# The head of a ternary 3x3 convolution: the weights loaded ahead of images 1 to 3, image 0's D, mean and variance taken ahead of the turning of the taps, image 1's mean and variance ahead of or between the first products

## What is computed

```python
max_val = jnp.max(jnp.abs(weight))
w_norm = weight / max_val                       # (1 where max_val is 0)
delta = 0.05 * jnp.max(jnp.abs(w_norm))
tern = where(w_norm > delta, 1, where(w_norm < -delta, -1, 0))
wq = where(tern > 0, Wp[0] * tern, where(tern < 0, Wn[0] * tern, tern))
...
g = x.reshape(B, 32, C // 32, H, W)
gn = ((g - mean(g)) / sqrt(var(g) + 1e-5)).reshape(x.shape)
out = x + conv3x3(gn, wq) + bias[None, :, None, None]
```

## Time and profile before

| | us |
|---|---|
| median of 3 runs | 574.85 (574.74 to 574.89) |
| time of the profiled execution | 575.64 |
| its span, first to last instruction | 574.0 |
| PE busy | 534.1 (93%) |
| DVE busy | 542.9 (95%) |
| ACT busy | 504.4 (88%) |
| POOL busy | 166.2 (29%) |

### The profile page before, as it was taken

The page is one execution under the profiler, slowest core; times in us unless marked ns, Lnnn a source line. Parts: engine busy times, 40 slices in busy tenths (PEclk is TensorE's granted clock), DMA queues, the critical chain, the costliest instruction groups (busy, mean ns, idle before and its releaser), DMA issues.

```text
span 574.0 us, 9367 instructions
## 1 busy us (share of the span) xinstructions
PE 534.1 (93%) x3238; PEld 320.1 (56%) x3238; DVE 542.9 (95%) x506; ACT 504.4 (88%) x485; POOL 166.2 (29%) x107
## 2 busy tenths in 40 slices
PE   0597999999999999999999999999999999999994
PEld 0453555555555555555555555565555555555552
...
DMA packets 28104, 153.43 MB, mean 267 GB/s; under 512 B 3504, under 2 KB 3504, under 8 KB 28080
## 3 DMA queue, kind: packets, MB, share of 16 engines
...
q10 hardware_dynamic: 576, 0.59, 0.3%
...
...
## 4 chain that ended last, share of the span: by engine, by line
DVE 68%; issue 24%; PE 4%; DMA 2%; DVEq 1%; ACT 1%; ACTq 0%
DVE parts L581 25%; DVE y L600 18%; DVE plane L541 10%; DVE plane L547 10%; DMA y<-in_L_conv_weight_dram 2%; PE even_rows L732 2%; DVE newton L570 2%; PE odd_rows L732 1%; DVEq L157 1%; DVE plane L553 1%; DVE neg_var L559 1%; ACT parts L386 1%; DVE rstd L565 0%; PE even_rows L697 0%; DVE parts L587 0%
## 5 line engine op out<-in xcount | busy, mean ns | idle before, releaser
L732 PE MATMUL odd_rows<-parts,w_lhsT 128*128 128x385 f16 (+1 forms) x1536 | 266.8, 330 | 8.6 <-DVE parts L581 7.5
L732 PE MATMUL even_rows<-parts,w_lhsT 128*128 128x385 f16 (+1 forms) x1536 | 267.6, 331 | 3.7 <-DVE parts L587 2.9
L581 DVE SCALAR_TENSOR_TENSOR parts<-plane,norm_scale,parts 128x1568 f16<-128x1568 f32 x127 | 233.4, 1842 | 4.3 <-ACT parts L386 4.3
L324 POOL TENSOR_TENSOR plane<-x 128x1512 f32<-128x1512 f32 x32 | 109.2, 3413 | 384.1 <-DVE parts L581 366.9
L732 PEld LDWEIGHTS even_rows<-parts,w_lhsT 128*128 128x128 f16 x1536 | 150.0, 98 | 111.9 <-issue 8.7
L732 PEld LDWEIGHTS odd_rows<-parts,w_lhsT 128*128 128x128 f16 x1536 | 148.1, 100 | 108.2 <-DVE parts L581 9.4
L386 ACT ACTIVATE parts<-plane,norm_scale 128x1568 f16<-128x1568 f32 x127 | 199.8, 1597 | 9.8 <-ACT plane L426 5.2
L432 ACT ACTIVATE junk<-x,negmean 128x3136 f16<-128x3136 f32 x32 | 92.9, 2904 | 0.0
L392 ACT ACTIVATE junk<-x 128x3136 f16<-128x3136 f32 x31 | 86.9, 2804 | 0.0
L600 DVE SCALAR_TENSOR_TENSOR y<-even_rows,out_scale,d_sb 128x784 f32<-128x784 f32 x62 | 61.0, 1025 | 0.0
L600 DVE SCALAR_TENSOR_TENSOR y<-odd_rows,out_scale,c_sb 128x784 f32<-128x784 f32 x62 | 60.9, 1023 | 0.0
...
## 6 DMA issues: line engine op xcount, KB each, us to landing
x<-in_x_dram SPq DMA_DIRECT2D x64, 784.0 KB, 11.7
...
y<-in_L_conv_weight_dram ACTq DMA_DIRECT2D x1, 576.0 KB, 10.7
wp_sb<-in_L_conv_Wp_dram ACTq DMA_DIRECT2D x1, 0.5 KB, 6.3
wn_sb<-in_L_conv_Wn_dram ACTq DMA_DIRECT2D x1, 0.5 KB, 7.9
...
```

The lines of the kernel that those rows point to most:

```text
L324: nc.gpsimd.tensor_tensor(plane[B][:, 0:PAIRS - 1, :], even[:, 0:PAIRS - 1, :], even[:, 1:, :], ALU.subtract).then_inc(plane_ready[B], 1)
L581: nc.vector.scalar_tensor_tensor(part(img, j, LO), plane[j][:], norm_scale[:, b_slice(img)], part(img, j, HI), ALU.mult, ALU.subtract).the ...
L732: ins = nc.tensor.matmul(product_ps(odd, b, b + 1)[:, 0, :, to:to + n], w_lhsT[:, prod, kw, :], part(img, prod, which)[:, b * BANK_ROWS:(b ...
```

## The change

The weights' DMA goes first in ACT's queue, ahead of Wp, Wn and the bias; SP issues image 0's loads and then waits for the weights before it issues those of images 1 to 3. DVE finds the local maximum, makes image 0's D and then the ternary weights; image 0's variance matmul stands ahead of the turning. ACT sums image 1 ahead of image 0's first high part, and PE's mean of image 1 stands behind the warm-up and ahead of all products. Image 0's A and B are both made by DVE, in the second slot; image 1's variance is taken in the middle of product D of image 0, and its A is moved to the third slot. The output scales and the comparison of Wp and Wn are placed anew, the negative weights are made only for the second pass, and the warm-up has 6 matmuls. Taps A and B are turned in other banks.

```diff
--- before.py
+++ after.py
@@
-WARM_UP = 11
+WARM_UP = 6
...
-            ps, bank = (odd_ps, 2) if j == B else (even_ps, j)
+            ps, bank = {C: (even_ps, 0), D: (even_ps, 1), A: (odd_ps, 1), B: (odd_ps, 2)}[j]
...
                             if img.buf != nxt.buf or img is nxt:
+                                if p == 0 and img is far:
+                                    sp.wait_ge(w_loaded, 16)
                                 load(img, 0, first=img is nxt)
                                 load(img, 1, first=img is nxt)
...
-                    if nxt:
-                        difference_b(nxt, after_c=now)
+                    if now and nxt:
+                        difference_b(nxt)
...
+            act.dma_start(w_raw, weight.rearrange("o i h w -> o (i h w)")).then_inc(w_loaded, 16)
             act.dma_start(wp_sb[:], wp.rearrange("(a b) -> a b", a=1).broadcast_to([P, 1])).then_inc(scalars_loaded, 16)
             act.dma_start(wn_sb[:], wn.rearrange("(a b) -> a b", a=1).broadcast_to([P, 1])).then_inc(scalars_loaded, 16)
-            act.dma_start(w_raw, weight.rearrange("o i h w -> o (i h w)")).then_inc(w_loaded, 16)
...
                         sum_squares(nxt)
                         edges(nxt)
                         root(nxt)
+                        sum_x(far)
                         make_first_hi(nxt)
                         make_hi(nxt, D)
+                    if second_slot:
+                        take_mean(nxt)
+                        sum_squares(nxt)
+                        make_hi(now, A)
+                        copy_c(now)
+                        make_hi(now, B)
+                        root(nxt)
+                        copy_d(now)
+                        make_hi(nxt, C)
                         sum_x(far)
-                    if now:
+                    elif now:
                         make_hi(now, A)
                         make_hi(now, B)
-                        if second_slot:
-                            take_mean(nxt)
                         copy_c(now)
-                        if second_slot:
-                            sum_squares(nxt)
-                        if nxt and not second_slot:
+                        if nxt:
                             root(nxt)
-                        if far and not second_slot:
+                        if far:
                             sum_x(far)
                         copy_d(now)
-                        if second_slot:
-                            root(nxt)
-                            sum_x(far)
...
+            def ternary_weights():
+                dve.wait_ge(w_max_turned, 1)
+                step(nc.vector.tensor_reduce(w_max[:], w_max_ps, AX_X, ALU.max))
+                step(nc.vector.tensor_scalar(col[0], w_max[:], 0.0, None, ALU.is_equal))
+                step(nc.vector.tensor_tensor(col[1], w_max[:], col[0], ALU.add))
+                step(nc.vector.reciprocal(col[2], col[1]))
+                nc.vector.tensor_scalar(w_raw, w_raw, col[2], None, ALU.mult)
+                step(nc.vector.tensor_scalar(col[3], w_max[:], col[2], THRESHOLD, ALU.mult, ALU.mult))
+                step(nc.vector.tensor_scalar(col[4], col[3], -1.0, None, ALU.mult))
+                dve.wait_ge(scalars_loaded, 32)
+                step(nc.vector.tensor_tensor(equal[:], wp_sb[:], wn_sb[:], ALU.is_equal))
+                step(nc.vector.tensor_scalar(neg, w_raw, col[4], equal[:], ALU.is_lt, ALU.mult))
+                nc.vector.scalar_tensor_tensor(pos, w_raw, col[3], neg, ALU.is_gt, ALU.subtract).then_inc(w_ternary, 1)
...
+                def make_first_b(img):
+                    plane_free(img, B)
+                    even = x_sb[img.buf][:, 0:H:2, :]
+                    nc.vector.tensor_tensor(plane[B][:, 0:PAIRS - 1, :], even[:, 0:PAIRS - 1, :], even[:, 1:, :],
+                                            ALU.subtract).then_inc(plane_ready[B], 1)
...
                 def emit(prev, now, nxt, far):
                     first_slot, second_slot = not now and not prev, now and not prev
                     if first_slot:
+                        if p == 0:
+                            local_max()
+                        make_d(nxt)
+                        if p == 0:
+                            ternary_weights()
+                        variance(nxt)
                         make_c(nxt)
-                        turned_weights((C, D))
-                        variance(nxt)
-                        turned_weights((A,))
                         first_rstd(nxt)
                         newton_factor(nxt)
                         scale_of_x(nxt)
-                        turned_weights((B,))
+                        turned_weights((C, D))
+                        make_first_lo(nxt)
+                    if second_slot:
+                        turned_weights((A, B))
+                        make_lo(now, D)
+                        make_a(now)
+                        make_first_b(now)
+                        variance(nxt)
+                        if p == 0:
+                            output_scales()
+                        make_lo(now, A)
+                        make_c(nxt)
+                        first_rstd(nxt)
+                        newton_factor(nxt)
+                        scale_of_x(nxt)
+                        make_lo(now, B)
                         make_d(nxt)
-                        make_first_lo(nxt)
-                        make_a(nxt)
-                    if now:
+                        make_lo(nxt, C)
+                    elif now:
+                        third_slot = prev.j == 0 and prev.q == p * N_IMG // X_BUFS
                         make_lo(now, D)
-                        if nxt and not second_slot:
+                        if third_slot:
+                            make_a(now)
+                        if nxt:
                             variance(nxt)
                         make_lo(now, A)
-                        if second_slot and p == 0:
-                            negative_weights()
-                    if now and nxt:
-                        make_c(nxt)
-                        make_d(nxt)
-                        if not second_slot:
+                        if nxt:
+                            make_c(nxt)
+                            make_d(nxt)
                             first_rstd(nxt)
                             newton_factor(nxt)
                             scale_of_x(nxt)
-                    if now:
                         make_lo(now, B)
-                    if now and nxt:
-                        make_a(nxt)
-                        if second_slot:
-                            variance(nxt)
-                            first_rstd(nxt)
-                            newton_factor(nxt)
-                            scale_of_x(nxt)
-                        make_lo(nxt, C)
+                        if nxt:
+                            make_a(nxt)
+                            make_lo(nxt, C)
...
                         if p == 0:
                             turn_max()
                         sum_first_mean(nxt)
-                        turn_weights()
                         pe.wait_ge(negmean_ready, nxt.count(plus=1))
                         sum_var(nxt, start=True)
+                        turn_weights()
                         warm_up()
+                        pe.wait_ge(var_ready, nxt.count(plus=1))
+                        sum_mean(far, start=True)
                     if second_slot:
-                        pe.wait_ge(w_ready, 4 * p + 4)
+                        pe.wait_ge(w_ready, 4 * p + 2)
                     if now:
                         if second_slot:
                             pe.wait_ge(half_lo_ready, p + 1)
@@ -766,18 +802,18 @@
                         multiply(now, C, 2)
                         multiply(now, C, 3)
                         wait(pe, odd_done, now.half(0))
-                        if second_slot:
-                            pe.wait_ge(var_ready, now.count(plus=1))
-                            sum_mean(nxt, start=True)
-                        elif nxt:
+                        if nxt and not second_slot:
                             sum_var(nxt, start=True)
                         pe.wait_ge(lo_ready[D], now.count(plus=1))
+                        if second_slot:
+                            pe.wait_ge(w_ready, 4 * p + 4)
                         multiply(now, D, 0)
                         multiply(now, D, 1)
-                        multiply(now, D, 2)
                         if second_slot:
                             pe.wait_ge(negmean_ready, nxt.count(plus=1))
-                        elif nxt:
+                            sum_var(nxt, start=True)
+                        multiply(now, D, 2)
+                        if nxt:
                             pe.wait_ge(var_ready, nxt.count(plus=1))
                         multiply(now, D, 3)
                         pe.wait_ge(lo_ready[A], now.count(plus=1))
@@ -786,15 +822,12 @@
```

(5 more changed lines are left out.)

45 lines of the change are left out of this document (21 added, 24 removed).

## The result

The changed kernel takes 566.77 us, the median of 4 runs (566.25 to 567.34), beside 574.81 us (574.74 to 574.89) for the kernel before; the ratio is 0.986, its 95% interval 0.9843 to 0.9877. The forecast was 566.3, in a range of 564.9 to 569.9. The profiled execution took 566.68 us over a span of 565.0.

The account below looks back on a forecast made before the run. DVE was taken as full from slot 1's middle to the end. Gains of 5.6 and 3.0 us took the span from 574.0 to 565.4, profiled time 567.0, less 0.79 for the median: 566.3 us, range 564.9 to 569.9.

Parts of the forecast that it names:

- Landing: DMA in the head: the weights land at 7.9 us (before 12.6) and the whole of image 0 at 9.8.
- my two bounds: Arrival of weights and whole image 0 by DMA: lower 7.1 and 9.1 us, upper 8.5 and 10.5.
- the loads come later: Rival, chance 0.14: image 1 or the weights arrive late by DMA; image 1 at 18.5 gives 568.3, weights at 10.4 cost 1.7.
- reference point: Start of DVE's low part of D of image 3: 86.85 us before the change, forecast 78.2.
- DVE to the ternary weights: Head on DVE: D(0) from 9.85 to 11.55, then the ternary chain; weights ready at 16.15 us, before 19.02.
- To the first product: Head on ACT and PE: first low half at 20.3, first product at 21.3 us (before 27.08), 5.6 us gained.
- First low half to the reference point: DVE's work from image 0's first low half to D(3)'s low part: 57.9 us, before 60.9, 3.0 gained.
- The new stall: In image 1's slot, DVE waits 1.65 us for ACT's high part of A after A(1) ends at 45.2.
- Sum: Whole kernel: 5.6 before the first product plus 3.0 after the first low half, 8.6 us off the span, to 565.4.
- The lower clock after the new wait: Rival, chance 0.15: PE idles from 47.7 to 49.9, then runs at half speed; about 3.0 us reach DVE, 568 to 569.7.
- No change: Rival, chance 0.02: in the slots, DVE is not what a slot waits for, so the time stays the same.
- slower: Rival, chance 0.02: in the head, image 1 queued behind the weights lands after 25.1 us, 17 us after issue.

Follow-up runs that it names:

- a_first_warm9: Changed kernel with plane A of image 1 made ahead of the low part of D in the third slot, and nine warm-up matmuls, not six; 564.55 us, ratio 0.9807.

## Why the prediction was right

*Landing.* Forecast 7.9 and 9.8, measured 7.6 and 9.4. Both lie between my two bounds, 0.3 and 0.4 us earlier than the middle that I took; the repeat of the same kernel landed at 8.2 and 10.0, so the middle lies between the two executions. The estimate beside it, by the Trainium skill, "DMA: Bandwidth & Descriptors", section "Anatomy of one DMA — SWDGE (gpsimd) path", was 8.0 for both together; the page gives its formula for DMAs issued by GpSimd, these were issued by SP and ACT, and 9.4 was measured. The rival "the loads come later" didn't come: nothing of PE waited for image 1's mean. The wait in SP's queue was not without effect, though; I had given it no gain, and without it the reference point comes 1.4 us later.

*DVE to the ternary weights.* Forecast 16.15, measured 15.69 (14.27 + 1.42), by the earlier landing. D(0) took 1.79, as I took it, and not 2.14.

*To the first product.* Forecast: squares done 15.6, variance 16.25, first low half 20.3, first product 21.3. Measured: 15.4, 16.10, 20.17, 21.35. The 0.4 of the earlier landing shrank on the way, since the mean matmuls and copies, an estimate of 1.15, took 1.38 (10.98 to 12.36). The mis-sized term here is the warm-up: 1.3 us forecast, 2.12 measured, since I scaled a row at the higher level and this one ran at the lower. It ends at 20.57 and the first product was wanted at 21.3, so the slack hid it.

*First low half to the reference point.* Forecast 57.9 us, measured 58.02 (78.19 - 20.17); low D(1) at 41.56 for 41.7, low D(2) at 61.57 for 61.6. The new stall, 1.65, came as forecast, and PE's wait behind it was 2.26 for the 2.2 between 47.7 and 49.9. In a_first_warm9, which makes A(1) ahead of the low part, that wait of DVE is gone.

*Slots.* 16.62 both before and after.

*Sum.* Forecast 8.6, measured 8.66 at the reference point, 9.0 in the span: the last output row of DVE starts 8.62 earlier (557.62 for 566.24), and the rest is the end of the stores. The profiled time is 566.68 where 567.0 was forecast. I then took off 0.79, since the median of before stood that far below its profile; after the change median and profile agree within 0.1 us. On the three chips of the experiments the kernel before has medians of 575.44 to 575.69, like its profile. Of the 28 executions there, seven have a mean granted clock of 0.992 or more and took 573.9 to 574.6 us; the others, at 0.990 or less, took 574.7 to 576.5. The profiled one (0.989, 575.64) is of the latter kind, with the 6.83 us at 0.50 of the earlier trace rows in it, while the four of the changed kernel are at 0.995 to 0.997. So about a microsecond of the gain counted from that profile is a stretch at the lower clock that not every execution of the kernel before has. To take 0.79 off the result as well was thus the wrong step, and it happened to be opposite in sign to the 0.3 that the sum was too careful; the result is 0.5 above the forecast.

*The rivals.* The lower clock after the new wait did occur, in one of two executions of this kernel, at some 0.65 us and not 3.0: it lasted 3.42 us where I had taken the 6.83 of the earlier trace rows whole, and the slack of PE took part. "No change" and "slower" were never near.
